# Last batch: a third score bank and a third maxima bank in place of two and four, and its maxima chunks spread evenly

## What is computed

```
x = x + tanh(g_x[0]) * attnA(layernorm(x), ctx)          # one head of 256, mask added
x = x + tanh(g_f[0]) * blockB(layernorm(x))              # 4 of 16 heads picked by a router
x = x + tanh(g_x[1]) * attnC(layernorm(x), ctx)          # 16 heads of 16
x = x + tanh(g_f[1]) * moeD(layernorm(x))                # 1 of 8 experts per row
```

```
scores = where(mask == 0, -1e9, q k^T / 4)               # 512 x 1601
attn = softmax(scores);  out = attn v
```

## Time and profile before

| | us |
|---|---|
| median of 3 runs | 2908.28 (2908.13 to 2912.55) |
| the profiled execution | 2907.62 |
| its span | 2905.9 |
| TensorE busy | 2680.9 |
| VectorE busy | 1737.9 |
| ScalarE busy | 1458.4 |
| the last batch's 208 steps | 184.25 |

### The profile page before, as it was taken

One profiled execution on the slowest core, in us unless ns is written; L12 is line 12 of the kernel. 1 busy time (PEld: TensorE's weight loads), 2 busy tenths in 40 slices (PEclk: granted clock), 3 DMA queues, 4 the chain that ended last, 5 costly groups with the idle time before them and its releaser, 6 DMA issues.

```text
span 2905.9 us, 39419 instructions
## 1 busy us (share of the span) xinstructions
PE 2680.9 (92%) x13624; PEld 1281.2 (44%) x13624; DVE 1737.9 (60%) x4230; ACT 1458.4 (50%) x2922; POOL 300.5 (10%) x352
## 2 busy tenths in 40 slices
PE   7878999999999999999999999999999889849998
PEld 3533433353334333443344333433353222229998
DVE  3446676667756776677657766776666677721111
ACT  2322575556554655456545654574556456613332
POOL 1200200020001100110002000200020000012222
PEclk9989999999999999999999999999999899969999
DMA  4421403232142313231324122403231222039996
GB/s 179 133 94 39 122 19 88 78 97 59 55 111 63 85 40 107 67 108 40 107 51 119 45 88 56 131 18 106 60 96 30 50 55 40 9 101 368 374 376 215
DMA packets 215140, 296.36 MB, mean 102 GB/s; under 512 B 50533, under 2 KB 180813, under 8 KB 214934
## 3 DMA queue, kind: packets, MB, share of 16 engines
q1 hardware_dynamic: 198428, 221.50, 27.3%
q0 software_dynamic: 16512, 72.32, 7.3%
HBM read 232.87 MB, written 60.50 MB: 101 GB/s over the span
## 4 chain that ended last, share of the span: by engine, by line
PE 78%; DVE 8%; ACT 6%; issue 5%; DMA 2%; SPq 1%; POOL 0%; ACTq 0%; POOLq 0%; DVEq 0%
PE PS L1443 12%; PE PS L1399 11%; PE PS L1426 10%; PE PS L1085 6%; DVE mxC L1904 6%; PE PS L1060 5%; PE PS L1569 5%; PE PS L1581 5%; PE PS L1114 3%; PE PS L1287 3%; PE PS L1181 2%; ACT reg L972 2%; PE PS L1204 2%; PE PS L1073 2%; PE PS L1196 2%
## 5 line engine op out<-in xcount | busy, mean ns | idle before, releaser
L972 ACT ACTIVATE reg<-PS 128x512 f32<-128x512 f32 (+1 forms) x1664 | 972.0, 598 | 969.9 <-PE PS L1426 964.0
L1904 DVE TENSOR_REDUCE mxC<-PS 128x1 f32<-128x400 f32 (+1 forms) x2048 | 1097.7, 570 | 567.1 <-PE PS L1399 554.3
L1399 PE MATMUL PS<-reg 96*128 96x400 bf16 (+1 forms) x2048 | 669.8, 340 | 65.5 <-DVE mxC L1904 37.8
L1426 PE MATMUL PS<-reg 99*128 99x512 bf16 (+1 forms) x1664 | 614.5, 385 | 38.0 <-ACT reg L972 29.6
L1399 PEld LDWEIGHTS PS<-reg 96*128 96x128 bf16 x2048 | 194.9, 98 | 586.6 <-DVE mxC L1904 447.2
L1443 PE MATMUL PS<-reg 128*17 128x512 f32 (+1 forms) x3328 | 442.0, 603 | 0.3 <-DVE reg L1928 0.3
L1426 PEld LDWEIGHTS PS<-reg 99*128 99x128 bf16 (+1 forms) x1664 | 163.4, 100 | 385.6 <-ACT reg L972 237.1
L1085 PE MATMUL PS<-reg 128*128 128x512 f32 (+1 forms) x416 | 211.6, 601 | 0.7 <-ACT reg L846 0.7
L1060 PE MATMUL PS<-reg 128*128 128x512 f32 (+1 forms) x512 | 206.2, 516 | 1.1 <-ACT reg L873 0.7
L1003 ACT ACTIVATE reg<-PS,reg 128x128 f32<-128x128 f32 x312 | 89.3, 369 | 217.7 <-issue 118.6
L1569 PEld LDWEIGHTS PS<-reg 128*128 128x128 f32 x1248 | 146.7, 193 | 3.1 <-issue 1.0
(11 more groups left out here) (214 smaller groups left out, 2569.1 us busy)
## 6 DMA issues: line engine op xcount, KB each, us to landing
reg<-in_D_W SPq DMA_DIRECT2D x78, 1024.0 KB
reg<-in_A_mask POOLq DMA_DIRECT2D x32, 800.5 KB, 6.0
dramK<-reg SPq DMA_DIRECT2D x144, 100.0 KB
dramV<-reg SPq DMA_DIRECT2D x48, 272.0 KB, 3.1
reg<-in_ctxT POOLq DMA_DIRECT2D x8, 1601.0 KB, 9.6
reg<-in_ctx POOLq DMA_DIRECT2D x8, 1536.0 KB, 7.6
dramQ<-reg SPq DMA_DIRECT2D x96, 128.0 KB
reg<-dramQ SPq DMA_DIRECT2D x32, 384.0 KB, 6.6
```

The source lines that it names most:

```text
L972: act.activation(pr[u % RING][0:r, :], PS[0:r, s_bank(v), :], ACT.Exp).then_inc(a_expC, 1)
L1399: last = mm(PS[:, bank, 0:w], qs[(NG * bb + g) % 3][0:ROWS, h, t * P:(t + 1) * P], ks[g % 2][0:ROWS, h, c0:c0 + w], start=True, stop=True)
L1426: last = mm(PS[0:r, bank, :], ks[g % 2][0:STK, h, c * P:c * P + r], qs[(NG * b + g) % 3][0:STK, h, :], start=True, stop=not with_mask)
L1904: v.tensor_reduce(mxC[:, h, t, j:j + 1], PS[:, m_ring(bb, g)[i % len(m_ring(bb, g))], 0:M_CH[j][1]], AX.X, ALU.max).then_inc(v_mx, 1)
```

## The change

In the last batch the digits of all groups come from one string, PIECES_END, with one or two chunks in every step from 1 to 44. The ring for maxima has three banks, (0, 1, 2), in place of four. From the first step of group 1 on, the scores go round three banks, (5, 6, 4), in place of two: a score then starts when the exponential three steps back is done. The first score that goes to bank 4 waits until VectorE has read the gate's logits of the batch before from it. The two matmuls for the ranking write bank 3 (F1) in place of bank 4.

```diff
-MB_END = MB + (F0, F1)
+MB_END, SB_END = MB + (F0,), SB + (F2,)
...
 PIECES = ("0001212322232223211111210112221321001111113300000000",
           "0002203232320132102231233322111111031002110100000000",
           "0001001211031002110222133323330021330113312300000000",
           "0000000000032223311121332223311121221122211320000000")
+PIECES_END = "0112121212121212121212211212121212112121212120000000"
...
-def chunks(g, v):
+def chunks(b, g, v):
+    pieces = PIECES_END if b == B - 1 else PIECES[g]
+    upto = [sum(int(d) for d in pieces[:w]) for w in (v, v + 1)]
...
-def s_bank(v):
-    return SB[v % 2]
+def s_bank(b, u):
+    if b == B - 1 and u >= UN:
+        return SB_END[(u - UN) % 3]
+    return SB[u % 2]
...
-                past(pe, a_expC, U - 1)
-                bank = s_bank(v)
+                if b == B - 1 and u >= UN + 3:
+                    pe.wait_ge(a_expC, U - 2)
+                elif b == B - 1 and u == UN + 2:
+                    pe.wait_ge(v_lg, B - 1)
+                else:
+                    past(pe, a_expC, U - 1)
+                bank = s_bank(b, u)
...
-                    mm(PS[:, F2, 0:TE * NE], lt, ohf, start=True, stop=True).then_inc(pe_rank, 1)
-                    mm(PS[:, F2, TE * NE:2 * TE * NE], onesD, ohf, start=True, stop=True).then_inc(pe_rank, 1)
+                    mm(PS[:, F1, 0:TE * NE], lt, ohf, start=True, stop=True).then_inc(pe_rank, 1)
+                    mm(PS[:, F1, TE * NE:2 * TE * NE], onesD, ohf, start=True, stop=True).then_inc(pe_rank, 1)
```

More of the change, by code:

```diff
@@ L64 @@
           "0000000000032223311121332223311121221122211320000000")
+PIECES_END = "0112121212121121212121211212121212112121212120000000"
 U_O1, U_O2, U_LD, U_XD, U_GATE = (8, 10), (13, 16), 18, (28, 30), 33
@@ L123, in rows @@
     return P if c < CT - 1 else CL
-def chunks(g, v):
-    upto = [sum(int(d) for d in PIECES[g][:w]) for w in (v, v + 1)]
+def chunks(b, g, v):
+    pieces = PIECES_END if b == B - 1 else PIECES[g]
+    upto = [sum(int(d) for d in pieces[:w]) for w in (v, v + 1)]
     return range(*upto)
@@ L971, in attend @@
                 past(act, pe_pv, UN * b + (u - RING) // GH + 1)
-                act.activation(pr[u % RING][0:r, :], PS[0:r, s_bank(v), :], ACT.Exp).then_inc(a_expC, 1)
+                act.activation(pr[u % RING][0:r, :], PS[0:r, s_bank(b, u), :], ACT.Exp).then_inc(a_expC, 1)
                 if v == 2 and g:
@@ L1419, in scores_t @@
                 c, h = v // GH, v % GH
-                r, U = rows(c), NU * b + UN * g + v
+                r, u = rows(c), UN * g + v
+                U = NU * b + u
                 if v == 0:
@@ L1457, in ahead_of @@
                 if g < NG - 1:
-                    return (b, g + 1, chunks(g, v)) if 0 <= b < B else (b, g + 1, ())
-                return (b + 1, 0, chunks(g, v)) if 0 <= b + 1 < B else (b + 1, 0, ())
+                    return (b, g + 1, chunks(b, g, v)) if 0 <= b < B else (b, g + 1, ())
+                return (b + 1, 0, chunks(b, g, v)) if 0 <= b + 1 < B else (b + 1, 0, ())
             def step(b, u, with_mask):
@@ L1973, in rank_early @@
                 dve.wait_ge(pe_rank, 2)
-                alone(v.tensor_copy(tot, PS[:, F2, TE * NE:2 * TE * NE].rearrange("p (t e) -> p t e", t=TE)))
+                alone(v.tensor_copy(tot, PS[:, F1, TE * NE:2 * TE * NE].rearrange("p (t e) -> p t e", t=TE)))
                 src, step_, n_pass = tot, 1, 0
@@ L1982, in rank_early @@
                 alone(v.tensor_tensor(tot, src, tot, ALU.subtract))
-                alone(v.tensor_tensor(tot, tot, PS[:, F2, 0:TE * NE].rearrange("p (t e) -> p t e", t=TE), ALU.add))
+                alone(v.tensor_tensor(tot, tot, PS[:, F1, 0:TE * NE].rearrange("p (t e) -> p t e", t=TE), ALU.add))
                 split_rank(0, TE, tot)
```

## The result

The changed kernel took 2897.23 us in the median of 8 runs (2894.26 to 2903.18), against 2908.2 us for the kernel before in 8 runs beside them (one of these took 5304.58 us and is left out of the ratio; without it the median is 2908.13). The medians are 11.0 us apart. The ratio is 0.9969, with a 95% interval of 0.9956 to 0.9982: 9 us less, between 5 and 13. The forecast was 2898.0.

The account below looks back on a forecast made before the run. Hand-overs between engines, not any one engine, were taken to bound the last batch. Groups 0 to 3 at +2.2, -3.0, -4.1 and -5.4 summed to -10.3 us, giving 2898.0 us on the median, range 2890 to 2904.

Parts of the forecast that it names:

- Group 3: Last batch's group without chunks: third score bank saves 4.8 us over ten trips and 0.6 in the head, -5.4 us.
- The loop named: Group 3: a trip's last score waits for the first exponential instead of the second, 2.87 to 2.39 us a trip.
- The rival with the ring of eight buffers: Group 3: exponentials' buffers, freed by the value matmuls, close the loop instead; 5.4 us fall away, 2903.4; chance 0.05.
- Groups 1 and 2, trips: Even pieces, three maxima banks: trips of 3.22 and 3.44 us, 29.6 us for nine, against 33.72 and 33.67.
- the rival "larger": TensorE's 3.0 us sets trips in groups 1 and 2, group 0 loses nothing: 7.8 us more, 2890.2; chance 0.17.
- Tails: Ends of groups 1 and 2: step 44's chunks put transposes 2.8 us after the value matmuls; 7.05 and 6.8 us.
- Group 0: First group: trips sum to 40.3 for 38.37 us, head and tail add 0.1 and 0.2; +2.2 us.
- the upper bound: Group 0: +5 us, if each of ten value-matmul sets pays the 0.48 us of a missing bank.
- Edits at nothing: Ranking's bank, gate-logits wait, K's second half, maxima row's DMA cost 0; some 8 us of ranking cover left.
- The sum: Whole kernel: 2.2 - 3.0 - 4.1 - 5.4 = -10.3 us, 2898.0 us on the median.
- The rival by count of banks: Seven banks used before and after, so no change, 2908; same time as "bank for bank", which had chance 0.04.
- The slower rival: Groups 1 and 2: chunks waiting for banks hold scores, ScalarE runs dry; +18 us, 2916; chance 0.09.

Follow-up runs that it names:

- e2: Changed kernel with the old digits, so three maxima and three score banks alone against the kernel before; median 2901.73 us, ratio 0.9987.
- e8: e7 with a fourth score bank in group 3; median 2882.73 us, ratio to the kernel before 0.9904.
- e3: Changed kernel with a fourth maxima bank (bank 3) given back, four and three banks, even digits; median 2887.63 us, ratio to before 0.9935.
- e6: Changed kernel with the two chunks of step 44 moved to steps 24 and 35; median 2895.03 us, ratio to before 0.9951.
- e5: Changed kernel with the old digits in group 0 of the last batch alone; median 2898.94 us, ratio to before 0.9975.
- e1: Even digits alone on the kernel before, four maxima and two score banks kept; median 2906.05 us, ratio 0.9992.
- e4: Kernel before with a third score bank (bank 4), four maxima banks and old digits kept; median 2895.63 us, ratio 0.9949.
- e7: e3, e5 and e6 in one kernel; median 2885.40 us, ratio to the kernel before 0.9925.

## Why the prediction was right

**Group 3: right.** 23.89 us for ten trips where 28.77 - 4.8 = 23.97 was forecast; the head 5.39, 0.3 less than forecast. The loop named was the loop: one bank took 0.48 us a trip from it (e2), one more 0.42 (e8). The rival with the ring of eight buffers fell with the trips of 2.38 us, and e8 goes below them with the same ring.

**Groups 1 and 2, trips: right.** 29.80 and 29.79 for a forecast of 29.6; trips of 3.23 and 3.45 for 3.22 and 3.44; that the ring of three makes them is shown by e3, which also gives TensorE's 2.99. So the rival "larger" (26.8 us) is what the kernel would do with four banks, and it fell here for the reason given against it.

**Tails: right.** 7.06 and 6.85 for 7.05 and 6.8, the transposes 2.81 us after V for 2.8, and e6 shows that the chunks of step 44 do it. The head of group 2, at full clock, came out 0.2 us above the 6.6 (6.83); the missing maxima bank makes some 0.75 us of a head (e3), which the prediction did not price.

**Group 0: the sum of the trips right by luck, the reason half wrong.** The nine trips took 40.36 us for a forecast of 40.3, but one by one they were 4.71, 4.72, 4.85, 5.46, 3.62, 4.59, 4.61, 4.10 and 3.71 us, where 5.4, 4.7, 5.4, 4.0, 4.4, 4.1, 4.9, 3.9 and 3.45 were forecast. Single trips were off by up to 1.5 us, and the errors cancelled. The largest is the fourth:

```profile
2395.12:2400.58 5.46, 3.75 (x23) 0.77 (x19) 5.43 (x17) 2.28 (x4) 1.02 (x1) 1.00 0.28 96
```

VectorE is busy 5.43 of its 5.46 us with reductions and with the statistics of the rows, which the prediction had put into the third trip. The step that priced the group also put the whole loss down to the places of the chunks, and the missing bank only into the upper bound. e5 shows 1.6 of the 2.0 us with the old digits. That the two costs do not add is measured; my reading, that a ring costs little where VectorE idles anyway, is not shown. With the head (7.31 us, forecast 6.6, 6.46 before, the bank again) and its tail at full clock (7.33) the group took 55.0 us, 3.0 more than before, where 54 and 2.2 more were forecast; in the profile itself it took 56.5.

**Edits at nothing: right.** Before its work after group 3 VectorE idled 8.72 us (13.82 before); the cover forecast was some 8:

```profile
2552.46 0.26 DVE L1935 RECIPROCAL rcC<-PS 128x16 f32<-128x16 f32 x1 [8.72 <-PE PS L1461]
```

No score that opens a group shows a wait for the row of maxima.

**The sum.** Forecast -10.3 us. The profiled batch shows -6.5; about 2.5 us of the gap is the clock (tail of group 0: 8.83 us, 7.33 in e1 and 7.32 in e3 without the dip; head of group 1: 7.82, against 6.83 in group 2), about 1.2 the heads of groups 0 to 2. Without the dip it would be -9.0, by groups +3.0, -2.7, -3.6 and -5.7 for a forecast of +2.2, -3.0, -4.1 and -5.4. By the cut of the table the changed kernel has -7.1, -9.6 without the dip, and e5, which has no dip, -9.9. The 9 us of the ratio and the 11.0 us between the medians agree with these within the interval of 5 to 13. The rival by count of banks, under which nothing would have changed, fell: seven banks were in use before and after, and 1 lies outside the interval of the ratio. Its mechanism is partly there all the same: the bank taken from the maxima costs 8.6 us against e3, and the change comes out ahead only because the even digits and the score bank bring more. And the count was no bad guide to what was left: the eighth bank brought 8.6 us on top of the change (e3), and 12.4 us or more on the kernel before (e4).

**The slower rival** did not come: ScalarE waited 11.1 us in the nine trips of group 1 where it had waited 13.6 before.

**The larger rival** also had group 0 lose nothing; it lost 3.0 us at full clock.

## What to carry to other kernels

Where three engines hand buffers round, write the loop of one period with its hand-over times for each ring, and move banks to the ring whose loop is longest, stage by stage; here a bank paid at most one reduction or one exponential (0.48 us) a period while its loop was the longest (0.48 in group 3 with e2; 0.3 with e3 and 0.42 with e8, where another need came first). Look first for a bank that lies idle in that stage: a third score bank from the idle one was worth 12.4 us by itself (e4), the exchange of banks 7.0 (e2), the even digits 6.0 to 7.3 alone (e1) and 4.3 on top of the idle bank (e3 against e4). Evening out the work needs no bank, and is worth doing beside it. The last pieces before a serial step (here the putting together of the maxima) paid by coming a step earlier, even though other trips got denser: 0.8 us a group (e6). Forecast a stage trip by trip, and check it trip by trip: a sum can be right with its terms wrong, as in group 0.

## What the runs showed of the hardware

The granted clock fell to its lower level for some microseconds at places that differ from run to run. In the profile of the changed kernel it happens at the end of group 0, after TensorE had waited 1.33 us for the transposes of the maxima (stretches of 2 us, columns as above):

```profile
2424.00:2426.00 2.00, 2.00 (x14) 0.62 (x15) 0.00 (x0) 1.06 (x2) 0.00 (x0) 0.85 0.00 0
2426.00:2428.00 2.00, 1.74 (x4) 0.26 (x2) 0.00 (x0) 1.30 (x3) 0.00 (x0) 0.50 0.02 6
2428.00:2430.00 2.00, 2.00 (x10) 0.17 (x9) 0.00 (x0) 0.85 (x2) 0.00 (x0) 0.50 0.31 56
2430.00:2432.00 2.00, 2.00 (x9) 0.57 (x5) 0.57 (x1) 1.26 (x3) 0.00 (x0) 0.50 1.10 197
2432.00:2434.00 2.00, 2.00 (x14) 0.67 (x14) 0.88 (x2) 1.17 (x3) 0.00 (x0) 0.94 1.09 213
```

0.50 of full speed is 1.2 GHz; the four value matmuls of this time took 1.91 us instead of 1.05. Longer waits for the same transposes in the tails of groups 1 and 2 of the same profile (1.85 and 1.63 us) went by at 1.00, and in e6 the dip lies in the middle of group 0 (a trip of 6.70 us at 0.74 and one of 5.79 at 0.50), in e8 at its start. A dip inside the last batch stands in six of the ten profiles (changed, e1, e3, e4, e6, e8), none in those of before, e2, e5 and e7. What sets one off stays open. It weighs as much as a small change: of the 8 runs of the changed kernel the three with a mean granted clock of 0.974 or 0.975 took 2902.29 to 2903.18 us, the five with 0.977 to 0.980 took 2894.26 to 2897.63. Stretches that ran at 1.00 repeat closely (the nine trips of groups 1 and 2 are 29.79 and 29.80 us in the changed kernel and in e5), so they separate 1.3 us where the medians could not separate 6.
